# ScalarE's two steps at the turn of a gated layer, in the other order

## The reference, cut to what matters

```
A = (adj != 0)
h = x
for l in range(5):
    m = h @ weight[l]
    agg = A^T @ m
    gi = agg @ w_ih.T + b_ih ; gh = h @ w_hh.T + b_hh
    r = sigmoid(i_r + h_r) ; z = sigmoid(i_z + h_z) ; n = tanh(i_n + r * h_n)
    h = (1 - z) * n + z * h
return layernorm(x + h * mask)
```

## Time and profile before

| | |
|---|---|
| median of three timed runs | 1930.01 us (1927.95 to 1930.7) |
| the profiled execution | 1934.07 us, span 1932.0 us |
| TensorE matmul busy | 1765.6 us (91%) |
| VectorE busy | 1514.8 us (78%) |
| ScalarE busy | 1172.8 us (61%) |
| GpSimd busy | 736.1 us (38%) |
| mean granted TensorE clock | 0.95 |

### The profile page before, as it was taken

How to read it: one execution, slowest core, us unless ns; L and a number is a source line. 1 busy time by engine, 2 the same in 40 slices (tenths; PEclk the granted TensorE clock), 3 DMA queues, 4 the chain that set the end, 5 groups by cost and what they waited for, 6 DMA issues and landing times.

```text
span 1932.0 us, 32634 instructions
## 1 busy us (share of the span) xinstructions
PE 1765.6 (91%) x11548; PEld 1354.2 (70%) x11548; DVE 1514.8 (78%) x3880; ACT 1172.8 (61%) x2738; POOL 736.1 (38%) x620
## 2 busy tenths in 40 slices
PE   4678999999999999999999999999999999999985
PEld 3345677777777777767777777767777777776663
DVE  3336689797978888797988889787988989788764
ACT  0233566767676666767666666757576666756552
POOL 1102244343434434443444344443434334333332
PEclk8568999999999999999999999999999999999997
DMA  2101000110101101110101011110111011010000
GB/s 68 31 12 26 23 19 24 32 28 18 42 18 32 28 17 27 30 30 18 42 17 32 16 28 29 29 31 17 32 29 25 19 32 29 18 28 17 12 6 11
DMA packets 105275, 49.26 MB, mean 25 GB/s; under 512 B 14725, under 2 KB 105114, under 8 KB 105114
## 3 DMA queue, kind: packets, MB, share of 16 engines
q1 hardware_dynamic: 105114, 47.18, 9.6%
HBM read 30.36 MB, written 8.39 MB: 20 GB/s over the span
## 4 chain that ended last, share of the span: by engine, by line
PE 73%; DVE 13%; ACT 5%; issue 3%; SPq 2%; DMA 1%; POOL 1%; POOLq 0%; DVEq 0%; ACTq 0%
PE RB L842 13%; PE RA L842 13%; PE RT L1015 8%; PE SS L936 7%; PE SS L811 5%; PE M L811 5%; PE RT L811 4%; PE M L954 4%; ACT e_s L520 2%; PE M L881 2%; PE M L875 2%; SPq L366 2%; DVE stats L616 2%; PE M L973 2%; DVE x L643 2%
## 5 line engine op out<-in xcount | busy, mean ns | idle before, releaser
L464 POOL TENSOR_TENSOR h_lo<-hT,h_hi 128x512 fp32r<-128x512 f32 x160 | 209.9, 1312 | 450.9 <-ACT h_hi L542 383.5
L520 ACT ACTIVATE e_s<-SS,s_ng 128x128 f32<-128x128 f32 x1024 | 277.3, 388 | 103.9 <-DVE s_ng L732 103.9
L432 POOL TENSOR_TENSOR rs<-ve,half_neg 128x4 f32<-128x4 f32 x128 | 155.6, 1215 | 351.2 <-DVE ve L621 351.2
L467 POOL TENSOR_TENSOR hd<-hT,nn 128x512 f32<-128x512 f32 x160 | 206.2, 1288 | 139.6 <-ACT nn L554 138.0
L554 ACT ACTIVATE nn<-tr,wT 128x512 f32<-128x512 f32 x160 | 117.0, 731 | 170.8 <-DVE tr L784 170.7
L776 DVE TENSOR_TENSOR agg_lo<-RT,agg_hi 128x512 fp32r<-128x512 f32 x160 | 110.2, 689 | 113.1 <-ACT agg_hi L545 110.8
L732 DVE TENSOR_REDUCE s_ng<-SS 128x8 f32<-128x1024 f32 x128 | 156.0, 1218 | 44.2 <-PE SS L936 44.2
L738 DVE TENSOR_TENSOR p_s<-SS,adjTe 128x512 f32<-128x512 f32 x256 | 165.2, 684 | 24.2 <-PE SS L811 22.4
L811 PE MATMUL SS<-ident,e_s 128*128 128x128 f32 x1024 | 145.9, 283 | 19.7 <-ACT e_s L520 19.7
L936 PE MATMUL SS<-km,qT 64*128 64x512 f32 x512 | 151.2, 668 | 13.6 <-DMA km<-kT 13.6
L780 DVE SCALAR_TENSOR_TENSOR un<-tr,un 128x512 f32<-128x512 f32 x160 | 118.5, 741 | 52.3 <-ACT un L551 52.3
(11 more groups left out here) (187 smaller groups left out, 4284.4 us busy)
## 6 DMA issues: line engine op xcount, KB each, us to landing
adjn<-in_adj_dram SPq DMA_DIRECT2D x32, 256.0 KB, 2.8
xin<-in_x_dram SPq DMA_DIRECT2D x32, 256.0 KB, 3.1
km<-kT SPq DMA_DIRECT2D x256, 32.0 KB, 2.0
adjr<-in_adj_dram SPq DMA_DIRECT2D x32, 256.0 KB, 3.0
out_dram<-x SPq DMA_DIRECT2D x32, 256.0 KB, 2.7
adjc<-in_adj_dram SPq DMA_DIRECT2D x128, 4.0 KB, 1.7
xs<-in_x_dram SPq DMA_DIRECT2D x128, 16.0 KB, 1.8
W1s<-in_L_gnn_W_dram SPq DMA_DIRECT2D x1, 640.0 KB
```

Of the source, the lines that this page charges most:

```text
L432: return pool.tensor_tensor(r[:, :], v[:, :], half_neg[:, 0, 0:GB], ALU.pow)
L464: pool.tensor_tensor(h_lo[g][:, :], hT[g][:, :], h_hi[g][:, :], ALU.subtract).then_inc(SG["h_lo"][g], 1)
L467: pool.tensor_tensor(hd[g][:, :], hT[g][:, :], nn[g][:, :], ALU.subtract).then_inc(SG["hd"][g], 1)
L520: ins = act.activation(e_s[:, h, :], S_[:, (h % GB) * P:(h % GB + 1) * P], ACT.Exp, bias=s_ng[:, h:h + 1])
```

## The change

In ScalarE's step "turn" of layers 1 to 4 the two instructions change places, each with its wait. The rounding of `hT` to `h_hi` comes first and waits for h_new; the copy of the transposes to `h_tok` comes second and waits for h_mm. Nothing else is changed.

```diff
                 elif kind == "turn" and k:
+                    wait_g(act, "h_new", g, it, k)
+                    act.activation(h_hi[g][:, :], hT[g][:, :], ACT.Copy).then_inc(SG["h_hi"][g], 1)
                     wait_g(act, "h_mm", g, it, k)
                     act.activation(cols(h_tok[g]), RT[:, :], ACT.Copy).then_inc(SG["h_tok"][g], 1)
-                    wait_g(act, "h_new", g, it, k)
-                    act.activation(h_hi[g][:, :], hT[g][:, :], ACT.Copy).then_inc(SG["h_hi"][g], 1)
```

## The result

The changed kernel took 1967.85 us, median of four runs (1964.97 to 1970.35), beside 1929.62 us for the kernel before: a ratio of 1.0198 (95% interval 1.0181 to 1.0216), 38.2 us more. Timed again later beside the experiments it took 1970.65 against 1928.97, a ratio of 1.0216 (1.0196 to 1.0235). The direction held, and so did the mechanism that the forecast had priced.

The account below looks back on a forecast made before the run. TensorE was taken to pace about 90 us of each 109.4 us turn, VectorE the other 20. Terms of 25.7 + 2.3 + 0.5 = 28.5 us on 1930.0 gave 1958.5 us, range 1944 to 1967.

Parts of the forecast that it names:

- both detours: Chain leaves TensorE for the VectorE stretch (1033.63) and a tanh (1079.73); both said to start from what TensorE delivers.
- A: Turn step at 1000.80 us: the next aggregation's eight weight loads end 0.48 us later.
- C: Turn step at 1019.50 us: the next aggregation's weight loads end 0.15 us later.
- E: Turn step at 1055.27 us, same pattern as A: 0.48 us later.
- F: Turn step at 1065.10 us: the next aggregation's weight loads end 0.38 us later.
- H: Turn step at 1083.66 us: h_tok and the weight loads behind it come 0.38 us later.
- Rival 1: Delay partly given back at the hand-overs to the VectorE stretch or the tanh: 1946 to 1950 us, chance 0.16.
- the gain side: Covering the transposes counted as 0 (at best 8 us); earlier h_lo 0 to -4.4 us.
- B: Turn step called free: h_tok 0.52 us later against 1.80 us of room.
- G: Turn step called free: h_tok 0.38 us later, ending at 1074.88, its loads beginning at 1075.45.
- the 2.3 us after 1760 us: End of the run: one more A, C and E (1.1 us) plus five cases of the last layers (1.2 us).
- Rival 2: Dearer: h_hi holds ScalarE its whole 0.63 us, or cases like C and G lose cover; up to 1966, chance 0.12.

Follow-up runs that it names:

- experiment 1: The changed kernel with one wait added, so GpSimd starts h_lo only when h_tok is done too: 1955.83 us, ratio 1.0124.
- experiment 2: The kernel before, h_tok still first, but h_lo of layers 1 to 4 about 0.5 us earlier, subtracting hT from itself: 1943.95 us, ratio 1.0058.
- experiment 4: The changed kernel with h_lo also waiting for h_tok and only half of h_hi rounded ahead of h_tok: 1938.54 us, ratio 1.0033.

## Why the prediction was wrong

- **The bound and the path held.** TensorE without idle time in three stretches of four, both detours starting from TensorE: the delays of A, C, E, F and H were handed on. Rival 1 (given back in part at the two hand-overs) fell for the steady turns: experiment 1's turn is 1.80 us longer for a sum of 1.87, and the step behind E gives 0.07 back in every turn.
- **The price of one case held.** 0.52 us of holding, 0.05 to the first load, 0.97 for eight loads gave 0.48, 0.15, 0.48, 0.38 and 0.38, and the trace shows 0.48, 0.15, 0.48, 0.39 and 0.38. With half of h_hi they scaled as they should. Over the whole kernel this part measured 23.1 us (21.5 to 26.7 by experiment 1's interval), not 28.5.
- **The step that failed is the gain side**, where the earlier h_lo was put at "0 to -4.4". I asked who waits for h_lo and found nobody; I did not ask what GpSimd's instruction does to VectorE while it runs. Where the prediction said of GpSimd's part that h_lo "is only released earlier", a collision was moved: L621 at F and L780 at B now start behind h_lo instead of ahead of it. The terms missed were 0.33 us (B) and 0.5 to 0.65 us (F) a turn, 12 to 14 us in 14 turns; the ratios of the changed kernel (either timing) and experiment 1 put them at 14 to 18 us, and experiment 2 alone showed 11. The forecast thus missed by 10 us where it had left out more than that, since the priced part came out 5 us smaller: the two errors pulled against each other.
- **The evidence was in the trace of before.** At B GpSimd's h_lo took 1.47 us instead of 1.27 beside VectorE's L780, in a row of the timeline that I had not chosen. L780 took over 0.8 us in 28 of its 160 instances, though its median is 0.69, and one of the 128 instances of L621 took 1.00 us (at 1830 us), where its median is 0.17. B and G were called free by looking at TensorE's room alone.
- **A smaller step failed too: the 2.3 us after 1760 us.** With the n-th instructions set against each other, the aggregations of layers 1 to 4 add 25.8 us between 250 and 1760 us in experiment 1 (the forecast had 25.7) and 3.3 us after that. But TensorE is no later at its last instruction than at 1760: 24.3 and 24.5 us against the second trace of before, and 33.1 and 33.1 for the changed kernel against the first. The gates' products (L842) give it back, 2.5 to 4.0 us. Before 250 us the aggregations add 0.3 to 1.6 us, depending on the pair of traces, for the 0.5 forecast.
- **Rival 2 had the sign and nearly the size** (up to 1966), for another reason: neither the 0.63 us nor a lost cover of C or G was at work. Its range did not include a second mechanism on top.
- **The signs named beforehand.** 98 waits for h_tok instead of 26 were close to the 75 or so more that were named, but their 37 us said nothing of the 14 us between the changed kernel and experiment 1. TensorE's busy time was to stand and its idle time to grow by the sum; on the pages the busy time grew by 17.0 us and the idle time by 16.2, so this sign didn't separate the two. The turn grew by 2.4 to 2.65 us against the second trace of before, and by 2.8 to 3.0 against the first, instead of 1.9. That was over the edge named as a sign of a dearer price, "above all at C and G"; but C cost its 0.15 and G nothing, and the excess stood at B and F.

What stays open: how the filling changes, since two traces of one kernel differ there by 7 us, in span by 4.5 (1932.0 and 1927.5) and by 0.38 us a turn; where the rest of the gap between the steps' sums and the measured 23.1 us of experiment 1 and 6 us of experiment 4 lies, beyond the end and the clock; and what brings the clock drops.

## What to carry to other kernels

An instruction that is released earlier is a change too, also when nobody waits for it: on GpSimd, look at what VectorE starts in the time that it moves into, and price a hold of VectorE at what is left of GpSimd's instruction (a little less here: 1.11 us with 1.26 left, 0.57 with 0.71 left), then take off what the engine behind it is late anyway. A case is free only if every engine that the moved work can hold has room, and a chain of ScalarE instructions without a gap behind it carries a delay to the engine that sets the pace, here 7 us later. Where an engine without idle time reads a buffer 0.05 us after it is ready, each 0.1 us put ahead of the producer costs 0.1 us; that part can be worked out from the rows to 0.01 us a case, as long as that engine sets the pace: in the last 170 us it was given back.

## What the runs showed of the hardware that was not expected

- A four-column VectorE operation of 0.17 us takes 1.28 us when a GpSimd operation on 128 x 512 started 0.01 us ahead of it, and 0.74 us when that one has half the columns. A hold goes both ways: GpSimd's 1.27 us became 1.47 where VectorE was first.
- Not every VectorE instruction is held: p_s (L738), which reads PSUM and one tensor in SBUF, took 1.29 us for two with h_lo beside it (847.79) and 1.27 us for two almost clear of it (858.73).
- GpSimd's subtraction took 1.04 us with one tensor as both inputs, 1.27 with two.
- The granted clock fell to 0.50 (1.2 GHz) for about 3 us in some turns, and not at the same turns in two executions of one kernel, though TensorE had been about as idle ahead of it in both (busy 1.03 of 3 us from 1040 us with the drop, 1.00 of 3 us at the same place without). TensorE's pieces took longer in the drop: four of L973 1.22 us instead of 0.71, four of L811 1.06 instead of 0.60. A turn of the second trace is 0.38 us longer than one of the first.
